# Adding the residual x where the experts' outputs are stored, and giving ScalarE the first product of the gated sum

## The reference

```python
x = x + L1_gnn(layernorm(x))                    # graph layer, 212500 edges
n = layernorm(x)
scores = router(n, edges)                       # 12500 x 4, graph attention
w = softmax over the two best scores            # the two others get weight 0
out = 0
for e in range(4):
    g = w of expert e, 0 where not chosen
    out = out + g[:, None] * (gelu(n @ W1[e] + b1[e]) @ W2[e] + b2[e])
return x + out
```

## Time and profile before

| what | us |
|---|---|
| median of 3 runs (lowest, highest) | 9162.32 (9157.47, 9171.59) |
| profiled execution, its own time | 9161.35 |
| span of that execution in the trace | 9159.1 |
| busy over the span: PE, DVE, POOL, ACT | 6907.0, 6371.8, 5142.5, 3316.0 |

### The profile page before, as it was taken

One profiled execution on the slowest core, in us unless ns is written; L12 is line 12 of the kernel. 1 busy time (PEld: TensorE's weight loads), 2 busy tenths in 40 slices (PEclk: granted clock), 3 DMA queues, 4 the chain that ended last, 5 costly groups with the idle time before them and its releaser, 6 DMA issues. The chain is left out here.

```text
span 9159.1 us, 86814 instructions
## 1 busy us (share of the span) xinstructions
PE 6907.0 (75%) x21757; PEld 3977.3 (43%) x21757; DVE 6371.8 (70%) x18821; ACT 3316.0 (36%) x7334; POOL 5142.5 (56%) x5327
## 2 busy tenths in 40 slices
PE   1536666666668999999998476776777769999984
PEld 1422322222224555555557233333333356666663
DVE  9967777777778877777765688888888881223238
ACT  1324434343343333333335344444444462222223
POOL 0157777777771100110443777777777567777774
PEclk9768888888889999999999677777777759999997
DMA  3256766766772000000225676777777672222337
GB/s 118 71 161 221 223 217 219 225 218 218 222 222 75 28 24 23 28 28 22 34 24 124 197 226 220 223 224 222 223 225 223 209 238 55 72 68 70 91 112 274
DMA packets 672166, 1355.19 MB, mean 148 GB/s; under 512 B 203371, under 2 KB 401870, under 8 KB 670642
## 3 DMA queue, kind: packets, MB, share of 16 engines
q0 software_dynamic: 238688, 579.40, 24.4%
q1 hardware_dynamic: 406352, 744.60, 23.1%
q10 hardware_dynamic: 26626, 25.65, 0.8%
HBM read 712.31 MB, written 649.65 MB: 149 GB/s over the span
## 5 line engine op out<-in xcount | busy, mean ns | idle before, releaser
L1274 POOL DMA_INDIRECT g_acc<-htab,g1sm_src x1760 | 1689.1, 960 | 538.0 <-issue 491.4
L1274 POOL DMA_INDIRECT g_acc<-htab,g0sm_src x1740 | 1649.8, 948 | 540.5 <-issue 488.5
L1384 PE MATMUL g1sm_sump<-g_acc,g1sm_to 128*128 128x264 f32 x3520 | 1482.5, 531 | 353.6 <-DVE g_acc L1529 326.4
L1384 PE MATMUL g0sm_sump<-g_acc,g0sm_to 128*128 128x260 f32 x3520 | 1314.4, 474 | 274.5 <-DVE g_acc L1529 231.8
L810 POOL DMA_INDIRECT g_acc<-rtab,k_f0bos x1024 | 997.4, 974 | 312.0 <-issue 306.2
L1384 PEld LDWEIGHTS g1sm_sump<-g_acc,g1sm_to 128*128 128x128 f32 x3520 | 661.4, 234 | 1130.0 <-DVE g_acc L1529 776.6
L1384 PEld LDWEIGHTS g0sm_sump<-g_acc,g0sm_to 128*128 128x128 f32 x3520 | 589.4, 209 | 962.0 <-DVE g_acc L1529 651.8
L2217 POOL DMA_DIRECT2D x<-g_acc x25 | 20.0, 800 | 1494.7 <-DVEq L2452 1353.5
L2636 DVE TENSOR_TENSOR k_arena<-g_bank,k_arena 128x512 f32<-128x512 f32 x196 | 135.6, 692 | 992.7 <-PE g_bank L2611 985.7
L1529 DVE TENSOR_TENSOR g_acc<-g_acc,g1sm_weightp 128x256 f32<-128x256 f32 x1760 | 708.4, 403 | 66.2 <-ACT g1sm_weightp L1318 66.2
L2348 PE MATMUL f_yp<-k_arena 128*128 128x256 f32 x3136 | 714.0, 380 | 13.0 <-DVE g_acc L2441 8.0
(11 more groups left out here) (462 smaller groups left out, 10660.2 us busy)
## 6 DMA issues: line engine op xcount, KB each, us to landing
sums<-k_arena SPq DMA_DIRECT2D x385, 528.0 KB, 3.5
sums<-k_arena SPq DMA_DIRECT2D x220, 520.0 KB, 3.1
sums<-g_acc SPq DMA_DIRECT2D x165, 520.0 KB, 4.2
z<-k_arena SPq DMA_DIRECT2D x96, 512.0 KB, 3.0
k_arena<-z SPq DMA_DIRECT2D x32, 1024.0 KB, 13.5
sums<-g_acc SPq DMA_DIRECT2D x55, 528.0 KB, 4.4
sums<-g0sm_now SPq DMA_DIRECT2D x55, 520.0 KB
g_acc<-htab,g1sm_src POOLq DMA_INDIRECT x1760
```

Source lines behind the costliest of these rows:

```text
L1274: nc.gpsimd.indirect_dma_start(slot[a][:, u, :], None, table, bass.IndirectOffsetOnAxis(ap=src[a][:, u:u + 1], axis=0)).then_inc(landed[a] ...
L1384: nc.tensor.matmul(bank(k, u), to[u // LOT % RING][:, u % LOT, :], slot[a][:, u, 0:W], start=True, stop=True).then_inc(summed, 1)
```

## The change

Each expert's stored output now holds x as well: DVE adds x to the finished `zs` buffer before `z_ready` is raised, with x loaded by SP one step ahead into a two-buffer ring (the room of `spent["x"]`). Since the weights of a node sum to 1, the gated sum of these outputs holds x once, and `choose_and_sum` loads no x. The first product gate0 * z0 becomes two 128x256 activations of ACT (`open_sum`), placed between `widen(n)` and `store(n - 2)`; DVE's `begin` keeps the second product only and waits for ACT's. The z ring has 15 buffers in place of 12, and `early` loads z of seven pairs in place of four. SP waits at the end of `finish_and_route` until the stores of x have landed.

```diff
@@ finish_and_route, sync
         sp.wait_ge(done, N)
+        for s in range(R):
+            sp.wait_ge(stored[s], 16 * len(range(s, N, R)))
@@ expert_outputs
-    SOON = 6
+    SOON = 7
+    xs = xroom.rearrange("p (q j d) -> p q j d", q=2, d=DIM)
+    xv = xin.rearrange("(b p) d -> p b d", p=P)
+    x_in = [c.sem(f"f1x_in{j}") for j in range(2)]
+    def load_x(sp, i, J):
+        sp.dma_start(xs[:, i % 2, 0:J, :], xv[:, i * CHUNK:i * CHUNK + J, :]).then_inc(x_in[i % 2], 16)
@@ sync: step
                 load(sp, i + 1, later)
+                load_x(sp, i + 1, later)
@@ sync, before the first step
+        load_x(sp, 0, CHUNK)
@@ vector: step, for each expert, after the two L2636
+                if e == 0:
+                    dve.wait_ge(x_in[i % 2], 16 * (i // 2) + 16)
                 dve.wait_ge(y_used, i * (2 * NE) + Q * (e + 1) + 2)
-                dve.sem_inc(z_ready, 1)
+                nc.vector.tensor_tensor(zs[e % 2][:, 0:J, :], zs[e % 2][:, 0:J, :], xs[:, i % 2, 0:J, :], ALU.add)\
+                    .then_inc(z_ready, 1)
@@ choose_and_sum
-    N, XS, YS, DS, LATE, SOON = NB // 2, 12, 4, 2, 2, 4
+    N, XS, YS, DS, LATE, SOON = NB // 2, 15, 4, 2, 2, 7
@@ early
-        for n in range(2 * step, 2 * step + 2):
-            load_x(sp, n)
-        if step < SOON:
-            load_z(sp, step)
+        load_z(sp, step)
@@ tensor
-            pe.wait_ge(x_in[s], 32 * (n // XS + 1))
+            pe.wait_ge(z_in[s], 16 * (n // XS + 1))
@@ scalar
+        def open_sum(n):
+            s = n % XS
+            act.wait_ge(z_in[s], 16 * (n // XS + 1))
+            if n >= YS:
+                act.wait_ge(done, n - YS + 1)
+            for j in range(2):
+                m = nc.scalar.activation(part0[n % YS][:, j, :], zs[s][:, j, 0:DIM], ACT.Identity,
+                                         scale=gate[:, 2 * n + j, 0:1])
+            m.then_inc(opened, 1)
...
                 widen(q, n)
+                open_sum(n)
                 if n >= LATE:
                     store(n - LATE)
@@ vector: begin
-            dve.wait_ge(x_in[s], 32 * (n // XS + 1))
-            if n >= YS:
-                dve.wait_ge(done, n - YS + 1)
-            for j in range(2):
-                m = stt(out=part0[n % YS][:, j, :], in0=zs[s][:, j, 0:DIM], scalar=gate[:, 2 * n + j, 0:1],
-                        in1=x[s][:, j, :], op0=ALU.mult, op1=ALU.add)
-            m.then_inc(opened, 1)
+            dve.wait_ge(z_in[s], 16 * (n // XS + 1))
             dve.wait_ge(opened, n + 1)
```

More of the change, by code:

```diff
@@ L2496, in expert_weights, with expert_outputs @@
     return w, issue
-def expert_outputs(nc, K, c, banks, turned, z, w, edges, room, placed, y_ready, early, late):
+def expert_outputs(nc, K, c, banks, turned, xin, xroom, z, w, edges, room, placed, y_ready, early, late):
     w1s, w2s, b2s, w_in = w["w1s"], w["w2s"], w["b2s"], w["w_in"]
@@ L2658, in expert_outputs, with choose_and_sum @@
     return first_rows, (sync, gpsimd, scalar, tensor, vector)
-def choose_and_sum(nc, K, c, banks, rsum, endi, has, H, NE, asn, adn, hn, bias, gamma, beta, xin, z, out, arena, rows, spare,
+def choose_and_sum(nc, K, c, banks, rsum, endi, has, H, NE, asn, adn, hn, bias, gamma, beta, z, out, arena, rows, spare,
                    turned, small, y_ready):
@@ L2684, in choose_and_sum @@
     y, part0 = pairs[:YS], pairs[YS:]
-    soon = list(cut(spare[0], [[2, NE * DIM]] * SOON + [[2, DIM]] * (XS - YS)))
-    x = soon[SOON:] + list(cut(spare[1], [[2, DIM]] * YS))
     *late_z, sq = cut(arena, [[2, NE * DIM]] * (XS - SOON) + [[most, F]])
-    zs = soon[:SOON] + late_z
+    zs = [*cut(spare[0], [[2, NE * DIM]] * (SOON - 1)), *cut(spare[1], [[2, NE * DIM]])] + late_z
     *diag, agg = cut(turned, [[2, NE - 2, P]] * DS + [[most, F]])
@@ L2703, in choose_and_sum @@
     sums_in = [c.sem(f"cssums_in{q}") for q in range(len(PARTS))]
-    x_in = [c.sem(f"csx_in{s}") for s in range(XS)]
+    z_in = [c.sem(f"csz_in{s}") for s in range(XS)]
     stored = [c.sem(f"csstored{s}") for s in range(YS)]
-    xv, zv = xin.rearrange("(b p) d -> p b d", p=P), z.rearrange("(b p) f -> p b f", p=P)
+    zv = z.rearrange("(b p) f -> p b f", p=P)
     ov = out[0:(NB - 2) * P, :].rearrange("(b p) d -> p b d", p=P)
-    def load_x(sp, n):
-        sp.dma_start(x[n % XS][:, :, :], xv[:, 2 * n:2 * n + 2, :]).then_inc(x_in[n % XS], 16)
     def load_z(sp, n):
-        sp.dma_start(zs[n % XS], zv[:, 2 * n:2 * n + 2, :]).then_inc(x_in[n % XS], 16)
+        sp.dma_start(zs[n % XS], zv[:, 2 * n:2 * n + 2, :]).then_inc(z_in[n % XS], 16)
     def early(sp, step):
@@ L2991, in gnn_two_layers @@
                     nc, K, g, banks, rsum, endi, has, H, NE, asn, adn, hn, a[f + "b_gat"], a[f + "ln_gamma"],
-                    a[f + "ln_beta"], xs[3], z, out, arena, places[:, 0:rows], (places[:, rows:], spent["t"]), spent["xT"],
+                    a[f + "ln_beta"], z, out, arena, places[:, 0:rows], (places[:, rows:], spent["t"]), spent["xT"],
                     spent["rden"], y_ready)
                 first_rows, (ex_sync, ex_pool, ex_act, ex_pe, ex_dve) = expert_outputs(
-                    nc, K, g, banks, turned, z, experts, edges, room, placed, y_ready, early, late)
+                    nc, K, g, banks, turned, xs[3], spent["x"], z, experts, edges, room, placed, y_ready, early, late)
                 fa_sync, fa_pool, fa_act, fa_pe, fa_dve = finish_and_route(
```

## The result

The changed kernel takes 9274.88 us (median of 4 runs, 9272.65 to 9278.02) against 9165.95 us for the kernel before on the same chip (4 runs, 9157.47 to 9171.59): 1.0122 times as long, 95% interval 1.0108 to 1.0135. Slower by 1.2%, 109 us; forecast were 9279 us and slower.

What follows compares the result with a forecast made beforehand. PE's cover in the expert stage, POOL's gathers setting its end, and DVE pacing the last stage were taken as bounds; 9161 + 90 (ring) + 27 (POOL) = 9278, 9279 us against the median; range 9243 to 9305.

Steps and rivals of the forecast that it cites:

- The ring: Last stage: ACT and DVE wait on each other in turn, 4.31 us a pair against 2.31, together +90 us.
- open_sum: Last stage, ACT's two new activations: 1.08 us, 0.99 after widen; bounds 0.60 and 1.20.
- the step from ACT to DVE: Last stage, handover from open_sum to DVE's second product: 0.04 us, taken from the step seen from DVE to ACT.
- The bounds of 72 to 100: Last stage: range of the ring's loss with the bounds of open_sum, +72 to +100 us.
- PE, loads, larger ring: Last stage: PE stays covered, loads fit at 304 GB/s, larger z ring and seven early pairs gain nothing.
- the x loads that vanish held up nobody: Last stage: dropping the loads of x gains nothing, since nothing waited for them.
- POOL: Expert stage: DVE's x adds, two SBUF inputs, hold POOL's edge gathers to their end; +27 us on POOL's end.
- the 27 us: Expert stage: two intervals of either kind per step, 2.62 us lost against 1.38 now, 1.24 x 22 = +27 us.
- nearly every add: Expert stage: with a gather every 1.249 us, nearly every 1.22 us x add catches one and holds it to its end.
- a gather needs something 0.12 us after its start: Gathers beside DVE products: about 0.12 us after starting, a gather needs something DVE holds until its instruction ends.
- the gather of the earlier trace: First mixture stage: gather starting at 2930.30 during DVE's 1.22 us product took 1.20 us, 0.26 above the median.
- PE hidden in the expert stage: Expert stage: PE hides DVE's 1.22 us add per expert, costed at nothing; without cover 120 us.

Runs made afterwards that it cites:

- ring: Changed kernel with ScalarE issuing each pair's store one pair later, store(n - 3) after open_sum(n), every instruction kept: 9204.47 us.
- dvefirst: Changed kernel with the first product back on VectorE as a product with a scalar, ScalarE's open_sum gone, x still added in the expert stage: 9194.92 us.
- noadd: Changed kernel with the 128x1024 add of x left out, loads of x kept: 9250.62 us.
- psum: Changed kernel with x copied by ScalarE into PSUM and added from there in two 128x512 adds per expert, one input in SBUF: 9252.51 us.
- split: Changed kernel with each add of x cut into two 128x512 halves, both inputs in SBUF: 9245.92 us.
- psumy8: Changed kernel with x added out of PSUM, the first product on VectorE and 8 buffers for finished pairs: 9167.97 us.
- psumy8e: Kernel psumy8 with an expert's edge work (highs, sums) in front of x's two adds on VectorE: 9154.54 us.

## Why the prediction was right

- *The ring.* Right as a mechanism, shown by ring. Its size was 83 us, not 90, and the term off was open_sum: sized 1.08 us for two from the earlier trace rows, where each activation had two operands per row to apply; it took 0.89, mean 0.49 each with a scale alone. It therefore added 0.79 us after `widen` and not 0.99, while the step from ACT to DVE took 0.10 us and not 0.04. That makes the pair 4.17 us (9130.26 to 9134.43), not 4.31. The bounds of 72 to 100 held.
- *PE, loads, larger ring.* They were costed at nothing, which is right here: DVE's products and adds wait for none of them. But "the x loads that vanish held up nobody" hides an effect: without them z loads crowd out the stores (dvefirst), some 11 to 13 us that the ring covered.
- *POOL.* The cause was right: +29.0 us between first and last gather, +27 forecast, and the adds make them (noadd), by their two inputs in SBUF (psum), each to the end of its instruction (split). The Trainium skill, "SBUF — State Buffer", section "Who interferes with whom", says that a VectorE instruction with two SBUF inputs contends with a GpSimd instruction that reads SBUF; these runs agree. Its probe, in which a `tensor_tensor` stalled no DMA, does not carry over to these gathers, which lost 28 us by such adds.
- *How the 27 us were counted.* Here luck helped. The prediction has an interval behind `highs` and one behind `sums` lose 1.28 us each. Summed over the trace, gathers lost 0.32 us in a mean interval behind `highs` and 2.02 behind `sums`, 7.8 and 46.5 us in all; the two errors cancel. Nor does "nearly every add" hold its gather: 33 of the 96 in the gathers' time did. In 60 cases a gather began between 0.12 us before and 0.04 us after the start of an add and lost nothing. By the prediction's reading, that a gather needs something 0.12 us after its start, these would have been held too; what the trace shows is that the one that began first, to within 0.04 us, went on. And the gather of the earlier trace rows was set against the median of another line; the median of its own, L1620, is 0.990 us, so it was stretched by 0.21 us and not by 0.26.
- *PE hidden in the expert stage.* Only nearly: the prediction looked at idle time on DVE and ACT and not at the edge rows that come later with POOL. DVE waited 62.2 us for them at L854, before the bias adds that PE and ACT need, and PE stood 18.9 us for ACT's gelu, a wait that the kernel before does not have; its last output matmul started at 8922.0 us, 24 later. It cost nothing only because POOL ended 30 us later still.

## What to carry to other kernels

Before moving work to an idle engine, write down both queues around it in order and follow who waits for whom once round: two engines that are each half idle can still take turns. What an instruction costs is also what it locks: two inputs in SBUF on VectorE, where GpSimd gathers, cost GpSimd's time. An operand in PSUM takes that hold away, and a shorter instruction shortens it, but either also moves the beat in which the gathers meet the next instructions, so the whole stage has to be counted again. A limit removed shows the next; here it was stores behind loads, cured by more buffers.

## What the runs showed of the hardware that was not expected

- A gather that starts up to 0.12 us before the add, or up to 0.04 us after its start, is not held (60 cases, 8048.79 for one). All 33 that started later inside an add, up to 0.14 us before its end, were held to that end and then took 0.81 to 0.84 us more.
- Scans that follow one another can hold a gather through many of them, 4.55 us in psum, or let it by between two; with the order of the same instructions changed, all gathers together took 20 us less (psumy8 1325.0, psumy8e 1305.0).
- Two DMA queues that both have work were served packet for packet (2126 and 2139 in dvefirst, 2364 and 2323 in the kernel before), whatever the packets' size: stores in 1 KB packets got 83 GB/s beside loads of 3.8 KB and 112 GB/s beside loads of 2.5 KB.
